# Hybrid attention and expert kernel: the skewed bias table in 16 copies, zeros in 2 KB rows, clears in the first two batches

## The reference

```python
def reference(x, ...):
    x = x + attn_a(layernorm(x))   # 16 heads of 8, q and k of unit length, softmax
    x = x + ffn(layernorm(x))      # 8 experts, top 2, at most C rows each
    x = x + attn_b(layernorm(x))   # 16 heads of 64, scores + position_bias, softmax
    x = x + ffn(layernorm(x))
    return x

# attn_b
values = rel_bias_table[buckets(mem - ctx)]       # (512, 512, 16): depends on mem - ctx alone
scores = einsum('bqhd,bkhd->bhqk', q, k) / 8 + transpose(values, (2, 0, 1))
# ffn, all 4096 tokens at once
gate, eidx = top_k(softmax(xf @ w_router), 2)     # gates divided by their sum
keep = position_within_expert < C                 # the others are dropped
y = sum over kept choices of gate * (relu(x @ w1[e] + b1[e]) @ w2[e] + b2[e])
```

## Time and profile before

| what | us |
|---|---|
| median of 3 runs (lowest, highest) | 1575.47 (1571.99, 1576.48) |
| span of the profiled execution | 1559.5 |
| TensorE busy, share of the span | 1274.3, 82% |
| VectorE busy | 933.7, 60% |
| ScalarE busy | 872.6, 56% |
| GpSimd busy | 508.7, 33% |
| attention A, from the start to the first load of the experts | 0 to 469 |
| first experts, to the first load of attention B | 469 to 541 |

### The profile page before, as it was taken

The page is one execution under the profiler, slowest core; times in us unless marked ns, Lnnn a source line. Parts: engine busy times, 40 slices in busy tenths (PEclk is TensorE's granted clock), DMA queues, the critical chain, the costliest instruction groups (busy, mean ns, idle before and its releaser), DMA issues. The chain is left out here.

```text
span 1559.5 us, 22437 instructions
## 1 busy us (share of the span) xinstructions
PE 1274.3 (82%) x6711; PEld 640.0 (41%) x6711; DVE 933.7 (60%) x2823; ACT 872.6 (56%) x1716; POOL 508.7 (33%) x787
## 2 busy tenths in 40 slices
PE   3888887878727479999899998999999998998193
PEld 2333332322215334454454454544544544545062
DVE  5345354444221168779878778698597787784210
ACT  1887576667503156666656656576466566562041
POOL 2002211222134512323533533434343335234245
PEclk7999798798658789999999999999999999998597
DMA  6265563357109525666656656666475665465062
GB/s 168 84 182 129 152 159 106 77 134 163 31 7 313 145 61 138 151 141 156 164 134 157 159 125 152 148 156 143 109 170 131 140 151 143 101 148 138 26 146 26
DMA packets 138040, 205.25 MB, mean 132 GB/s; under 512 B 35406, under 2 KB 80413, under 8 KB 137920
## 3 DMA queue, kind: packets, MB, share of 16 engines
q1 hardware_dynamic: 109952, 146.01, 37.2%
q0 software_dynamic: 27392, 56.76, 16.9%
q10 hardware_dynamic: 576, 1.05, 0.2%
HBM read 61.75 MB, written 46.58 MB: 69 GB/s over the span
## 5 line engine op out<-in xcount | busy, mean ns | idle before, releaser
L1480 ACT ACTIVATE tile<-tile,low 128x512 f32<-128x512 f32 x512 | 364.3, 715 | 269.5 <-DVE low L1567 268.6
L1267 POOL DMA_DIRECT2D crossed<-blocks x512 | 252.9, 502 | 545.1 <-DVE blocks L1580 495.8
L1567 DVE CUSTOM_DVE_ANT_0 tile<-s_ps,bias 128x512 f32<-128x512 f32 x512 | 330.6, 682 | 45.3 <-PE s_ps L1344 35.0
L599 ACT ACTIVATE probs_a<-score_ps,gbound 128x1024 f32<-128x1024 f32 x256 | 269.5, 1113 | 135.2 <-PE score_ps L845 107.7
L1344 PE MATMUL s_ps<-kT,qT 64*128 64x512 f32 x1024 | 272.6, 638 | 34.3 <-DVE low L1567 32.6
L1580 DVE STREAM_TRANSPOSE blocks<-tile 128x512 f32<-128x512 f32 x384 | 256.8, 694 | 0.0
L1364 PE MATMUL o_psb<-crossed,v_b 128*64 128x512 f32 x512 | 238.5, 609 | 5.7 <-DMA crossed<-blocks 5.6
L859 PE MATMUL o_ps<-probs_a,v_ext 128*32 128x512 f32 x1024 | 159.6, 701 | 0.5 <-ACT probs_a L599 0.5
L336 POOL DMA_INDIRECT slots<-rows_r,slot_r x128 | 126.2, 986 | 83.7 <-DVE slot_r L279 43.8
L1344 PEld LDWEIGHTS s_ps<-kT,qT 64*128 64x128 f32 x1024 | 87.3, 190 | 152.0 <-issue 88.1
L845 PE MATMUL score_ps<-q_stack,k_stack 32*128 32x512 f32 x512 | 103.6, 563 | 53.0 <-ACT probs_a L599 38.2
(11 more groups left out here) (159 smaller groups left out, 1622.1 us busy)
## 6 DMA issues: line engine op xcount, KB each, us to landing
crossed<-blocks SPq DMA_DIRECT2D x512, 96.0 KB
crossed<-blocks POOLq DMA_DIRECT2D x512, 96.0 KB
inv_row<-inv_rows SPq DMA_DIRECT2D x128, 128.0 KB
q_parts<-parts SPq DMA_DIRECT2D x32, 256.0 KB, 3.6
k_stack<-k_parts SPq DMA_DIRECT2D x32, 256.0 KB, 4.1
q_stack<-q_parts SPq DMA_DIRECT2D x32, 256.0 KB, 4.8
bias_skew<-bias_rows SPq DMA_DIRECT2D x8, 1024.0 KB
w_f<-in_w SPq DMA_DIRECT2D x32, 256.0 KB, 5.4
```

The costliest lines, as they stand in the source:

```text
L599: nc.scalar.activation(probs[q % 2][:, c % 4 // 2, pair:pair + 2, :].rearrange("p h t -> p (h t)"), score_ps[c % 2][:, :], ACT.Exp, bias=g ...
L1267: pool.dma_start(strip_to(n, a, m), strip_from(n, a, m)).then_inc(crossed_sw[n % 2], 16)
L1480: nc.scalar.activation(tile[(b * NS + k) % RING][s][:, :], tile[(b * NS + k) % RING][s][:, :], ACT.Exp, bias=low[n % 2][:, s, i:i + 1], sc ...
L1567: nc.vector.tensor_tensor_reduce(out=tile[(b * NS + k) % RING][s][:, :], in0=s_ps[k % 2][s][:, :], in1=bias[:, h, off:off + S], scale=1.0, ...
```

## The change

`bias_skew` has 17 rows for each head, of which 16 are written, in one transfer (`spread_bias`) in batch 0, after the wait for that batch's stacks. The bias table is loaded by 8 transfers instead of 16: the n-th fills partitions 16n to 16n+15 for all 16 heads, from the same copies with another start. The pieces have 896 numbers as before, and their number is the same.

`y_odd` is zeroed from a tile of its own, `zeros`, which GpSimd sets at its start, and each partition writes 2 KB in one row; the eight transfers (`clear_y`) stand in batch 1, ahead of the parts of batch 2. The blank rows of `slots[1]` are written after batch 1. The counts that are waited for follow the number of transfers.

```diff
+COPIES = 16
...
+        zeros = sb("zeros", [P, TB * D])
...
-            def clears(b):
-
-                if b == 0:
-                    sp.wait_ge(table_sb, 2)
-                    sp.sem_inc(g["passed_sp"], 1)
-                    sp.wait_ge(zero_ready, 1)
-                    sp.sem_inc(g["passed_sp"], 1)
-                sp.dma_start(g["bias_skew"][:, bass.ds(b * (P // B), P // B), :],
-                             g["rows"][:, :].unsqueeze(1).to_broadcast([HEADS, P // B, REL])).then_inc(cleared, 16)
-                blank(1, b, cleared)
-                sp.dma_start(g["y_odd"].rearrange("(b t p) d -> b p t d", b=B, p=P)[b],
-                             g["blank"][:, 0, 0:D].unsqueeze(1).to_broadcast([P, TB, D])).then_inc(cleared, 16)
+            def spread_bias():
+
+                sp.wait_ge(table_sb, 2)
+                sp.sem_inc(g["passed_sp"], 1)
+                sp.dma_start(g["bias_skew"][:, 0:COPIES, :],
+                             g["rows"][:, :].unsqueeze(1).to_broadcast([HEADS, COPIES, REL])).then_inc(cleared, 16)
+
+            def clear_y():
+
+                for n in range(B):
+                    sp.dma_start(g["y_odd"].rearrange("(b p r) d -> b p (r d)", b=B, p=P)[n], zeros[:, :]).then_inc(cleared, 16)
...
                 if before:
                     store_x(b - 1)
+                if b == 0:
+                    spread_bias()
+                if b == 1:
+                    clear_y()
                 parts_to_dram(b + 1)
                 stacks(b + 1)
-                clears(b)
...
             batch(0, False)
+            sp.wait_ge(zero_ready, 2)
             for n in range(B):
                 blank(0, n, slots_clear)
-            for b in range(1, B - 1):
+            batch(1, True)
+            for n in range(B):
+                blank(1, n, cleared)
+            for b in range(2, B - 1):
                 batch(b, True)
-            clears(B - 1)
             store_x(B - 2)
             store_x(B - 1)
-            sp.wait_ge(cleared, 16 * 3 * B)
+            sp.wait_ge(cleared, 16 * (1 + 2 * B))
...
+            nc.gpsimd.memset(zeros[:, :], 0.0).then_inc(zero_ready, 1)
...
-                flat = g["bias_skew"].rearrange("h p r -> h (p r)")
-                for h in range(HEADS):
-                    row = flat[h, P - 1:P - 1 + P * (REL - 1)].rearrange("(p r) -> p r", r=REL - 1)[:, 0:WREL]
-                    sp.dma_start(wb["bias"][:, h, :], row).then_inc(wb["loaded"], 16)
+                flat = g["bias_skew"].rearrange("h c r -> h (c r)")
+                for n in range(P // COPIES):
+                    low = P - 1 - n * COPIES
+                    part = flat[:, low:low + COPIES * (REL - 1)].rearrange("h (p r) -> p h r", r=REL - 1)[:, :, 0:WREL]
+                    sp.dma_start(wb["bias"][n * COPIES:(n + 1) * COPIES, :, :], part).then_inc(wb["loaded"], 16)
...
-        g["bias_skew"] = nc.dram_tensor("bias_skew", (HEADS, P, REL), F32, kind="Internal").ap()
+        g["bias_skew"] = nc.dram_tensor("bias_skew", (HEADS, COPIES + 1, REL), F32, kind="Internal").ap()
```

More of the change, by code:

```diff
@@ L1298, in _ @@
         def _(pe):
-            pe.wait_ge(g["wb"]["loaded"], 16 * (4 + HEADS))
+            pe.wait_ge(g["wb"]["loaded"], 16 * (4 + P // COPIES))
             def rows_T(b):
@@ L1663, in _ @@
             norm_rows(0)
-            dve.wait_ge(g["wb"]["loaded"], 16 * (4 + HEADS))
+            dve.wait_ge(g["wb"]["loaded"], 16 * (4 + P // COPIES))
             dve.wait_ge(r.const, 4)
```

## The result

The changed kernel takes 1590.19 us (median of 4 runs, 1583.31 to 1592.78) beside 1573.73 us of the kernel before (4 runs, 1566.12 to 1576.48). The ratio is 1.0127, with a 95% interval of 1.0078 to 1.0176: slower by 12 to 28 us, 16.5 by the medians. A second group of runs on another chip gave 1.0135 (1.0065 to 1.0204). The forecast was 1615, so +40: the sign and the place were right, the size was not.

The account below looks back on a forecast made before the run. The path through the first experts' last scatter was taken to set attention B's start. Span 1559.5, less 5 in batch 7, plus 45 for held-up scatters, gave 1599.5; with 16.0 around it 1615.5 us, range 1588 to 1640.

Parts of the forecast that it names:

- GpSimd's start memset, cost 0: Start of attention A: GpSimd's 128x512 memset takes 0.55 us and fits its 0.60 us wait; cost 0, 0.1 at most.
- Batch 1, cost 0 to 2: Attention A: eight y clears (6.5 us) fit the 10 us between x_mid and q_parts; cost 0, at most 2 us.
- Batch 7, gain 5 (0 to 10): Attention A: without clears GpSimd's 8.6 us scatter wait goes, TensorE gains its 4.6 us; 5 taken, range 0 to 10.
- The load at 104 GB/s: First experts: table load into 16 partitions at a time runs at 104 GB/s, so 70.6 us, ending at 566 for 518.5.
- Scatters held up, one after each piece, +45: First experts: one GpSimd scatter passes per 8.8 us table piece, so attention B starts 45 us later.
- the bound of 32: First experts: scatters let through row by row, ending with the table, so attention B starts 32 us later.
- Attention B unchanged: Attention B, some 930 us, has nothing of this edit in it and only starts later.
- 16.0 us around the span: Whole kernel: 16.0 us between the profiled span of 1559.5 and the median of 1575.47, carried unchanged.
- The prediction's own sign: Whole kernel: a time between 1590 and 1602 would make the hold-up of the scatters wrong.
- rival 2: First experts: only queue order counts or scatters pass row by row; 24.5 to 32 us later, 1595 to 1602; 18%.

Follow-up runs that it names:

- each_batch: Changed kernel with each load taking every eighth partition, and y clears and second-slot blanks spread over batches 1 to 6; ratio 1.0009 to the kernel before.
- early_clears: Changed kernel with 128 copies and the old table load, bias-row spreads sent in batches 0 to 6, none in batch 7; ratios 0.9942 and 0.9948 to before.
- load_only: Kernel before plus only the new table load (8 transfers of 16 partitions and all heads); 1551.55 beside 1525.17 us, ratio 1.0168.
- after_again: The changed kernel, unchanged, run and traced again on another chip; ratio 1.0135 to the kernel before.
- half_rows: Changed kernel with each of the 8 table loads cut into two of half the row (1792 bytes for 3584); ratio 1.0067 to the kernel before.
- wide35: Changed kernel with 35 copies, the table loaded by heads over all 128 partitions, source in 4 steps of 32 rows; ratio 1.0141 to before.
- strided4x32: Changed kernel with 32 copies and 4 loads of 32 partitions, each taking every fourth partition; ratio 0.9952 to the kernel before.
- wide16x8: Changed kernel with 23 copies, the table loaded by heads over all 128 partitions, source in 16 steps of 8 rows; ratio 0.9957 to before.
- wide_load: Changed kernel with 23 copies, the table loaded by heads over all 128 partitions, source in 8 steps of 16 rows; ratio 0.997 to before.

## Why the prediction was right or wrong

**GpSimd's start memset, cost 0:** right; the first load of stacks is at 33.33 us, before at 33.20.

**Batch 1, cost 0 to 2:** right for the clears themselves, for which nothing waits. But after comes 3 to 8 us late to batch 7, a cost that the sum has nowhere, and each_batch shows that the place of the clears isn't its cause. Over 33 to 367 us the granted clock is 0.89 in both traces of before, 0.86 in both of after and 0.85 in early_clears. That the lower clock is what costs these us fits the rows and wasn't tested. On load_only's chip there is no such lateness: batch 7's stacks come at 343.6 us in load_only, and at 341.1, 347.8 and 340.5 in the three with the new clears.

**Batch 7, gain 5 (0 to 10):** right in sign and place, and in the number partly by luck. The net gain of attention A is 3.7 and 6.0 us, early_clears without any new load has 6.3, and its time is 8 us under before's. Of the working, the first part is confirmed (wait for the scatters 8.6 to 1.3 us). But batch 7 itself got 9 to 12 us shorter on these chips, twice the 5, and the late start took the rest back.

**The load at 104 GB/s:** the cause was right, and the range of rates too (102 to 349). The value was too low by a tenth: 116 GB/s over all of it, 121 in a stretch of after_again. The rows it was taken from were reads, of 4 KB rows; the write into 16 partitions was 12% faster. That is 63.2 us for 70.6, the largest part of what the next term has too much.

**Scatters held up, one after each piece, +45:** this is the step that failed. The term of the sum measured +35.3 and +29.3 us, 32.3 on average. The mechanism put down for it was wrong: q0 gets a packet in each turn, row by row, as the bound of 32 had it, and half_rows shows that the pace follows the row's length. The Trainium skill's turn of some 9 to 17 descriptors (DMA: Bandwidth & Descriptors, "Queues, rings and completion order"), which the prediction took for support, is not what these rows show: 214 packets to 214, one of 3.3 KB and one of 0.5 KB on average, and even microsecond by microsecond. By pieces an expert would take 26 us; measured are 13.1.

Yet the model left the same two experts (6 and 7) for after the table's end as the trace shows, so this mistake alone cost little of the size. The difference of 10 us between 45 and 35.3 is made up so: the table was 7.4 us shorter; expert 6 was issued 0.5 us ahead of the table's end and not 2.5 behind it, since nothing had piled up, 3.0; 0.3 in the last two experts; less 0.7 for a later start. The bound "row by row, 32, ending with the table" has nearly the measured size by luck. Its table was those 7 us too long, and its other half was wrong: since an expert then takes 13.1 us, two are left at the end.

**Attention B unchanged:** not quite. It is 2.7 and 6.0 us shorter in after, and on load_only's chip it goes down as the first experts get longer (924.6 us at 75.8, 924.8 at 81.0, 923.0 at 92.0, 921.6 at 103.0). The two traces of before alone differ by 3.5 us. The difference goes with TensorE's clock: its 4128 matmuls there are busy for 836.2 and 835.9 us in before and for 829.9 and 831.6 in after, at a granted clock of 0.95 and 0.96 over the stage, and on load_only's chip for 829.4, 828.0, 826.7 and 823.3 us in the order above. TensorE had been idle longer ahead of it; that this is why the clock was granted more was not tested. (wide35 has 948.9, but there B itself waits at its start: the first inv_rows is issued 43 us into it, 28 to 31 in the others.)

**16.0 us around the span:** wrong. Every run lies 1.7 to 1.8 us over its own span. The profile of before was of an execution of some 1561 us, 14 under the median shown. It didn't change the +40, which was added to the median.

Together: -5 + 45 was forecast; the stages gave -4.9, +32.3, -4.4 and +0.5 on average, so +23.5, beside +16.5 and +21.1 by the medians. What lies between the stages and the medians is the choice of the profiled executions, that of before above all. The prediction's own sign, a time between 1590 and 1602 for a wrong hold-up of the scatters, pointed at the right step. The right neighbour was rival 2 (row by row, 1595 to 1602), whose range misses the median by 5 us.

## What to carry to other kernels

In these runs the rate of a load followed which partitions it touched, and not how many, and copies in memory bought freedom there: with every fourth partition, 32 copies load as fast as 128 (327 GB/s), while 32 neighbours get two thirds of it (203). Where a slow transfer shares the engines with another queue's small ones, look at its row length: each row was one turn here, and the other queue paid one turn for each of its packets. Work that nothing waits for can still hold up transfers that are waited for: with the clears out of batch 7 (and the y clears in 2 KB rows) the kernel got 0.5% faster, without a change of the load.

## What the runs showed that was not expected

- The best of all is early_clears, 0.9942 and 0.9948, beside strided4x32 at 0.9952 and wide16x8 at 0.9957; the intervals overlap, and all three are faster than both kernels.
- How much the outermost step of a source is worth, by the number of engines that it leaves: 8 steps ran with the engines 42.8% busy at 164 GB/s, 4 steps 21.2% at 81 GB/s, 16 steps 89.0% at 262 GB/s.
- While the narrow spread was *read*, q0 got nothing for 5 us; beside the narrow *write* it got one packet in two. Why they differ was not tried; the prediction's model was taken from the read.
- The last scatter's landing, not the table's end, closes the block in the traces, even in half_rows and wide_load, where the two fall within 2 us of each other (at about 520 and 502); only in wide35 was it SyncE, which issued the table's loads until 559.8.
